# A first expert plan from nine of twelve token tiles, and four full expert tiles run while the last tokens are routed

## The reference

```
h = h + attn(layernorm(h))        # along axis 0 of 1536 tokens, 12 heads of 16
x = layernorm(h)
t = rmsnorm(x) * norm_scale
g = t @ gate_w.T + gate_b                 # 16 experts
top_vals, top_idx = top_k(g, 4)
route_w = softmax(top_vals)
hid = t @ mlp1_w + mlp1_b                 # 192 -> 768 per expert
a = glu * sigmoid(1.702 * glu) * (lin + 1)    # glu = min(., 7), lin = clip(., -7, 7)
y = a @ mlp2_w + mlp2_b                   # 384 -> 192
out = h + x + sum over the 4 experts of route_w * y
```

## Time and profile before

| what | value |
|---|---|
| median of 3 runs | 701.22 us (701.01 to 701.29) |
| profiled execution, own time | 701.36 us |
| its span, first to last instruction | 699.1 us |
| mean granted clock of PE | 0.955 of full |
| busy: PE, DVE, ACT, POOL | 618.1, 397.4, 382.1, 284.4 us |
| attention with its head start | from 213 to 432 us of the span |
| from attention's last matmul to the experts' first | 432 to 458 us |
| experts | 458 to 679 us |

### The profile page before, as it was taken

How to read it: one execution, slowest core, us unless ns; L and a number is a source line. 1 busy time by engine, 2 the same in 40 slices (tenths; PEclk the granted TensorE clock), 3 DMA queues, 4 the chain that set the end, 5 groups by cost and what they waited for, 6 DMA issues and landing times.

```text
span 699.1 us, 17374 instructions
## 1 busy us (share of the span) xinstructions
PE 618.1 (88%) x5055; PEld 424.5 (61%) x5056; DVE 397.4 (57%) x1418; ACT 382.1 (55%) x733; POOL 284.4 (41%) x340
## 2 busy tenths in 40 slices
PE   5888899889795999999999998579999999999980
PEld 5776687568662222222222323379999999999970
DVE  0445857775665236666666646636666666666650
ACT  0323347533334899999999997034444444444430
POOL 3122323321424034666666645603445353544451
PEclk9999999999997999999999999579999999999995
DMA  8999999700015525655565330289898998889944
GB/s 318 420 364 312 318 326 348 261 2 1 12 41 132 85 122 184 167 160 160 160 167 160 70 79 33 87 272 279 239 250 235 237 250 236 245 236 240 244 62 79
DMA packets 78193, 132.63 MB, mean 190 GB/s; under 512 B 36859, under 2 KB 62892, under 8 KB 76876
## 3 DMA queue, kind: packets, MB, share of 16 engines
q1 hardware_dynamic: 64892, 116.79, 53.7%
q0 software_dynamic: 11712, 14.19, 10.9%
q10 hardware_dynamic: 1552, 1.18, 0.5%
HBM read 105.53 MB, written 58.42 MB: 235 GB/s over the span
## 4 chain that ended last, share of the span: by engine, by line
PE 60%; DVE 15%; POOL 7%; issue 7%; ACT 5%; DMA 3%; SPq 1%; DVEq 0%; POOLq 0%; ACTq 0%
PE ps L1039 13%; PE ps L1068 8%; PE ps L1049 7%; PE ps L889 7%; PE ps L876 5%; PE ps L720 2%; PE ps L729 2%; POOL rstd L516 2%; DVE stat L1267 1%; ACT mid L1174 1%; DVE mid L1279 1%; PE ps L750 1%; ACT big L1174 1%; ACT big L1130 1%; PE ps L836 1%
## 5 line engine op out<-in xcount | busy, mean ns | idle before, releaser
L1174 ACT ACTIVATE mid<-ps 128x1536 f32<-128x1536 f32 x108 | 153.8, 1467 | 11.0 <-PE ps L876 10.4
L1039 PE MATMUL ps<-mid,big 128*128 128x128 f32 x756 | 99.2, 282 | 0.7 <-ACT mid L1200 0.7
L666 POOL DMA_INDIRECT out<-mid x32 | 49.6, 1550 | 118.4 <-ACT mid L1219 117.1
L876 PE MATMUL ps<-mid 52*128 52x512 f16 x432 | 86.5, 390 | 11.8 <-DMA mid<-big 5.6
L1039 PEld LDWEIGHTS ps<-mid,big 128*128 128x128 f32 x756 | 92.0, 194 | 5.0 <-ACT mid L1200 1.4
L1210 ACT ACTIVATE mid<-mid 128x384 f32<-128x384 f32 x63 | 33.0, 523 | 100.5 <-DVE mid L1618 100.5
L889 PE MATMUL ps<-mid 128*32 128x384 f32 x864 | 85.9, 501 | 0.0
L1618 DVE TENSOR_SCALAR mid<-ps,big 128x128 f32<-128x128 f32 x189 | 54.7, 345 | 48.0 <-issue 35.4
L1068 PE MATMUL ps<-big,mid 128*128 x378 | 67.5, 327 | 0.9 <-issue 0.5
L1068 PEld LDWEIGHTS ps<-big,mid 128*128 128x128 f32 x378 | 60.6, 190 | 1.7 <-issue 1.6
L876 PEld LDWEIGHTS ps<-mid 52*128 52x128 f16 x432 | 16.8, 94 | 72.8 <-ACT mid L1174 36.2
(11 more groups left out here) (232 smaller groups left out, 1073.1 us busy)
## 6 DMA issues: line engine op xcount, KB each, us to landing
big<-w_cat SPq DMA_DIRECT2D x63, 576.0 KB, 4.5
expert_in<-expert_in SPq DMA_DIRECT2D x16, 1774.5 KB, 46.4
big<-expert_in SPq DMA_DIRECT2D x63, 136.5 KB, 3.7
w_cat<-w_a SPq DMA_DIRECT2D x4, 1536.0 KB, 7.3
big<-w SPq DMA_DIRECT2D x2, 2304.0 KB, 8.9
big<-patches SPq DMA_DIRECT2D x8, 512.0 KB, 8.9
big<-patches SPq DMA_DIRECT2D x2, 2048.0 KB, 21.7
w_cat<-w_b SPq DMA_DIRECT2D x2, 1536.0 KB, 7.4
```

The source lines that it names most:

```text
L666: nc.gpsimd.indirect_dma_start(sums[r], bass.IndirectOffsetOnAxis(ap=tok_idx[q], axis=0), yt[q], None, compute_op=ALU.add).then_inc(y_out[ ...
L876: last = nc.tensor.matmul(SETS[kb % 2][:, c * 512:(c + 1) * 512], keysT[n_par][row:row + STK, kb * P:(kb + 1) * P], qrysT[n_par][row:row + ...
L1039: last = nc.tensor.matmul(banks[half][:, c * P:(c + 1) * P], w1_t[q][:, half * FF + c * P:half * FF + (c + 1) * P], xtT[r][:, 0:P], start= ...
L1174: nc.scalar.activation(probs[kb % 4], SETS[kb % 2], ACT.Exp, scale=0.5).then_inc(probs_ready, 1)
```

## The change

A first plan is made from the counts of token tiles 0 to 8. It lists four tiles of 128 rows (`T0 = 4`) that are already full then. They are loaded during the last attention tile and run between the end of attention and the rest of the plan; the late plan lists the other 59. There are still 63 expert tiles in all. `xtT`, `glu`, `lin`, `sig`, `actv` and `yt` move to other places in SBUF, as attention still uses the old ones; the biases use banks 5, 6 and 7; the sums of the first four tiles all go to `odd_sum`. The RMS norm's root is taken from the variance along with the layer norm's, in one power of two columns, so that the square and its sum fall away.

```
 def root_var(r):
-    step(tensor_scalar(vps[:, 0:1], var, 1e-5, None, ALU.add))
-    tensor_tensor(rstd[:, 0:1], vps[:, 0:1], nhalf[:, 0:1], ALU.pow)
+    tensor_scalar(vps[:, 0:1], var, LN_EPS, None, ALU.add)
+    step(tensor_scalar(vps[:, 1:2], var, 1.0 + RMS_EPS, LN_EPS * RMS_EPS, ALU.mult, ALU.add))
+    tensor_tensor(rstd[:], vps[:], nhalf[:, 0:2], ALU.pow)
-root_ms: one tensor_scalar and one pow on POOL; norm_square: square and reduce_sum on DVE
...
 DVE, behind dve_head(NT - 2):
+dve.wait_ge(plan_consts, 1)
+memset, then 15 instructions: full0 = counts of full tiles, ends0 = their running sum,
+at most T0; plan0_cols = expert and row                       -> plan0_cols_ready
 tT_copy(base)
 output(NT - 2, base + 1)
 choose(NT - 3, base + 2)
+first_tables(base + 3)                                        # -> plan0_ready
...
 norm_rows(NT - 1, 1, (NT - 1) // 2)
+clip_glu(0, 0)
 tT_copy(base + 1)
+clip_lin(0, 0)
 choose(NT - 1, base + 2)
+clip_act(0, 0)
 weigh(NT - 1, 1)
 place(NT - 1, 1, base + 3, cnt)
 the plan (two instructions more than before)                  # -> plan_cols_ready
+clip_glu(1, 1); clip_lin(1, 1); clip_act(1, 1)
 the tables                                                    # -> plan_ready
+clip_glu(2, 0); clip_lin(2, 0); clip_glu(3, 1); clip_lin(3, 1)
 six bias adds
+clip_act(2, 0); clip_act(3, 1)
...
 PE, last attention tile, behind the values of block 3:
+plan_transpose(plan0_cols, plan0_cols_ready, base + 3)
 PE, behind attention (all new order):
+x_transpose(0, 0, 16)
+comb_transpose(range(0, 4), 5)
+out_transpose(NT - 1, base - 1)
+x_transpose(1, 1, 16)
+ranks(NT - 2, base)
+comb_transpose(range(4, 8), 6)
+mlp1(0, 0, 16)
+mlp1(1, 1, 16, narrow_first=True)
+t_transpose(NT - 1, 1, base + 1)
+x_transpose(2, 2, 16); comb_transpose(range(8, 10), 5)
+logits(base + 2)
+x_transpose(3, 3, 16)
+mlp1(2, 2, 16)
+ranks(NT - 1, base + 3, counts=True)
+mlp2(0, 0)
+mlp1(3, 3, 16, narrow_first=True)                             # waits lin_ready >= 2
+mlp2(1, 1)
+comb_transpose(range(NT - 2, NT), 5)
+plan_transpose(plan_cols, plan_cols_ready, base + 4)
+six weighted_bias, the last three each wait for a bias add
+mlp2(2, 0); mlp2(3, 1)
+x_transpose(4, 0, 32); x_transpose(5, 1, 32); two_tiles(4, 0, 16); two_tiles(6, 2, 16)
...
 SP:
-sp.wait_ge(plan_ready, 1)
+sp.wait_ge(plan0_ready, 1)
 load_weights(0, 0)
+sp.wait_ge(rows_out[0], 16 * (TOPK * 5 + 1)); sp.wait_ge(rows_out[1], 16 * (TOPK * 4 + 1))
 rows and weights of tiles 0 to 3
+sp.wait_ge(plan_ready, 1); load_weights(NW, 0)
+wait for all rows_out, then tiles 4 and on
```

More of the change, by code:

```diff
@@ L48 @@
 HROW = P // 2
+T0 = NW
 DUMP = NT * P
@@ L317, in head_base, with plan_entry, x_bank, sum_of @@
             return 4 * n - 6 if not isinstance(n, int) or n >= 2 else 1
+        def plan_entry(first, late, j):
+            if isinstance(j, int) and j < T0:
+                return first[0:1, j:j + 1]
+            return late[0:1, bass.ds(j - T0, 1)]
+        def x_bank(j, q):
+            return 0 if isinstance(j, int) and j < T0 else 7 * (q % 2)
+        def sum_of(j):
+            return 1 if j < T0 else j % 2
+        def adds_to(s, j):
+            return sum(1 for i in range(j) if sum_of(i) == s)
         def held_wait(eng, s, value):
@@ L921, in ranks, with plan_transpose @@
                 last.then_inc(tr_ready, 1)
+            def plan_transpose(cols, ready, job):
+                pe.wait_ge(tr_taken, job)
+                pe.wait_ge(ready, 1)
+                for c in range(2):
+                    last = nc.tensor.matmul(b7[0:1, c * P:(c + 1) * P], cols[:, c:c + 1], ident[:], start=True, stop=True)
+                last.then_inc(tr_ready, 1)
             def pe_head(n, par, old=True, last=False):
@@ L974, in _, with comb_transpose @@
             pe_head(NT - 1, 1, last=True)
-            base = head_base(NT - 1) + 7
-            out_transpose(NT - 1, base - 1)
-            for t in range(NT - 2):
-                last = nc.tensor.transpose(ps[0:E, t * P:(t + 1) * P], comb_all[:, t, :], ident[:])
-            last.then_inc(combT_psum, 1)
-            ranks(NT - 2, base)
+            base = head_base(NT - 1) + 8
+            def comb_transpose(tiles, b):
+                for i, t in enumerate(tiles):
+                    last = nc.tensor.transpose(bank(b)[0:E, i * P:(i + 1) * P], comb_all[:, t, :], ident[:])
+                last.then_inc(combT_psum, 1)
             def weighted_bias(pair):
@@ L1215, in y_tile @@
                 if before is not None:
-                    act.wait_ge(y_out[q % 2], before)
+                    act.wait_ge(y_out[1 if isinstance(j, int) and j < T0 + NW else q % 2], before)
                 act.wait_ge(y_psum, j + 1)
@@ new lines, in _ @@
+            clip_glu(1, 1)
+            clip_lin(1, 1)
+            clip_act(1, 1)
+            dve.wait_ge(tr_ready, base + 5)
+            nc.vector.tensor_copy(ej_i, b7[0:1, 0:MT])
+            nc.vector.tensor_copy(row_i, b7[0:1, P:P + MT])
+            nc.vector.tensor_scalar(exrow_i, b7[0:1, 0:MT], float(P), None, ALU.mult).then_inc(tr_taken, 1)
+            dve.wait_ge(tr_taken, base + 5)
+            nc.vector.tensor_copy(bank_mark[:], ones[:, 0:1]).then_inc(plan_ready, 1)
+            clip_glu(2, 0)
@@ new lines, in _ @@
+            clip_lin(2, 0)
+            clip_glu(3, 1)
+            clip_lin(3, 1)
+            dve.wait_ge(base_ready, NT)
+            for t in range(0, NT, 2):
+                dve.wait_ge(bias_psum, t // 2 + 1)
+                pair = h_res[:, t:t + 2, :].rearrange("p t c -> p (t c)")
+                nc.vector.tensor_tensor(pair, pair, bank(BIAS_BANK[t // 2])[:, 0:2 * C], ALU.add).then_inc(bias_added, 1)
+            clip_act(2, 0)
+            clip_act(3, 1)
+            for j in range(T0, 2 * NW):
```

394 lines of the change are left out of this document (227 added, 167 removed).

## The result

The changed kernel takes 707.17 us (median of 4 runs, 704.70 to 708.83), the kernel before 701.25 beside it; the ratio is 1.0068, with a 95% interval from 1.0045 to 1.0091. It is slower by 0.7%, clear of noise. The profiled execution is the fastest of the four: 704.70 us, span 702.8, granted clock 0.961.

The account below looks back on a forecast made before the run. ACT was taken to pace attention, with PE nearly full, and PE the experts' steady part. 701.36 + 8.0 + 14.1 - 17.2 = 706.3, less 0.14 for the median: 706.1 us; range 699.5 to 711.5.

Parts of the forecast that it names:

- Term A: Last attention tile: its last PE matmul, called T, comes 8.0 us later, at least 5.3.
- the stall: Last attention tile: DVE's first plan, waiting for POOL's `edges`, delays out_transpose and leaves ACT idle, 4.8 us.
- the clock: Last attention tile: PE at half clock behind its idle time costs 2.7 us, between 0 and 5.
- Term B: Gap from T, attention's last PE matmul, to the first left-over expert tile: 14.1 us longer, at least 11.3 at full clock.
- The adds: In the gap: DVE's six bias adds, the last three waiting for banks of the first, take 3.5 us.
- mlp2(2) and (3): In the gap, behind clip_act(2): the second matmuls of expert tiles 2 and 3 take 1.95 us for both.
- Rival 3: PE at half clock through the whole gap: some 4 us more there, 2.5 more behind it, 712 us; chance 0.15.
- rival 1: The clock stays full in the last attention tile and the gap: 700.6 us, give or take 1.5; chance 0.2.
- Term C: Experts from the first left-over tile to tiles 8 and 9: 12.6 us instead of 29.8, saving 17.2 us.
- the norm is worth nothing in either place: Shorter routing norm gains nothing: beside ACT's exponentials in attention, or in the gap, where PE is busy until T + 7.75.
- wrong if T stays under 436: Sign against the forecast: attention's last PE matmul, expected at about 440 us in the trace, coming before 436.
- The table load: In the gap: ACT's 1.28 us load ahead of tile 0's swish makes DVE wait ahead of the last `weigh`.

Follow-up runs that it names:

- e8: The changed kernel with the routing norm of the kernel before, so the plan alone: 709.58 us, ratio 1.0104 to the kernel before.
- e1: The changed kernel with POOL making the table `edges` before attention instead of behind four indirect DMAs: 700.15 us, ratio 0.9968 to the kernel before.
- e3: The changed kernel with 36 unused identity transposes on PE ahead of the late out_transpose of token tile 10: 703.24 us, ratio 1.0014 to the kernel before.
- e2: The kernel before with only the routing norm changed to one power of two columns: 697.68 us, ratio 0.9940.
- e10: e9 with clip_act(0) behind the plan's columns, mlp2(0) behind the plan's transposes, third bias pair behind mlp1(3): 693.24 us, ratio 0.9890 to the kernel before.
- e9: e1 with half the biases early, mlp1(4) ahead of mlp2(2) and (3), and e4's edit: 691.15 us, ratio 0.9863 to the kernel before.
- e4: The changed kernel with the late plan's transpose ahead of mlp1(3) and DVE's tables ahead of tile 1's clips: 707.36 us, ratio 1.0077 to the kernel before.
- e12: e9 with 18 and 22 unused identity transposes in PE's idle time ahead of mlp1(3), two bias pairs behind them: 689.90 us, ratio 0.9818 to the kernel before.
- e11: e10 with unused identity transposes on PE ahead of mlp1(3), 30 before the first biases and 15 behind mlp2(0): 692.24 us, ratio 0.9866 to the kernel before.

## Why the prediction was right, and where it was not

**The sum held: 707.17 measured, 706.1 forecast.** But it held in part by luck: two of its errors cancelled, as the two halves show.

**Term A** (8.0 forecast). The mechanism was as told, from the IOTA to ACT's wait. ACT's waits in the last token tile grew from 0.7 to 7.8 us, by 7.1, in the changed kernel and in e8 alike. Against e1 the stall costs 4.0 us in the first wait (4.22 less 0.24) for 4.8 forecast, since the sixteen instructions took 2.7 us (415.21 to 417.92) and not 3.3; the clock costs 2.7 (e3) for 2.7; against before, the plan's transposes cost 0.42 for 0.5. Attention as a whole is 5.8 us longer in the changed kernel and 7.4 in e8: the difference is what the norm gives in the other token tiles.

**Term B** (14.1 forecast, 17.0 measured by the distance from T to mlp1(4)). Up to the bias adds the steps held: mlp1(3) took 4.3 us for 4.0, plan_ready was at T + 26.8 for 28.0, the first bias add at T + 31.9 for 32.5. Then two terms were mis-sized. The adds took 5.3 us (467.84 to 473.15), not 3.5: I counted waits for banks but not that PE makes each product at half clock. And mlp2(2) and (3) took 3.85 us, not 1.95. Rival 3, half clock through the whole gap, had 0.15. It came true in part: mlp2(1), the plan's transposes and the first three pairs of biases ran at full clock (1.14, 0.60 and 2.18 us), but from 467 to 477 us the clock was 0.50, and the two terms above add 3.7 us, where the rival had some 4 for the gap. mlp1(4) then ran at full clock, so that the 2.5 us that it added behind stayed away. The bound of 11.3 for B at full clock is not worked out in the prediction: mlp1(3) at full clock takes off 1.7 us, which gives 12.4, and rival 1 should have stood 1.1 us higher.

**Term C** (17.2 forecast): 29.83 less 12.28, 17.55.

**The step that failed** is "the norm is worth nothing in either place". It gave 0.0036 to 0.0060 of the time, 2.5 to 4.2 us (e8, e2). In the other token tiles I took ACT's exponentials to cover it, but ACT waited for scores there, and with the new norm these waits shrank from 3.1 to 1.7 us. In the gap I argued that PE, busy until T + 7.75, would hide the earlier row. PE, free at T + 6.9, did hide most of it: t_transpose came only 0.5 us sooner than in e8. What I left out is DVE's own order: clip_glu(0) stands behind the norm's rows, started 1.4 us sooner, and with it everything behind, up to mlp1(4), 2.1 us sooner than in e8. The plan alone costs 1.0104, 7.3 us; by the steps of the forecast it was 4.9. In e8's trace the excess is in B, 19.0 us (44.87 less 25.84) for 14.1. So the plan was underpriced by 2.4 us and the norm's gain left out, of about the same size.

**What would show it**: "wrong if T stays under 436". T was 435.97, and the step it guarded was right; the tokenizer ahead had run 1.9 us shorter. The bound belonged on a length, not on a time of the trace. The table load was forecast on the path and was: DVE waits 1.11 us for it. The Trainium skill's drain of 1.38 us ("ScalarE: Activation LUTs", What ACT_TABLE_LOAD costs) would by the prediction's estimate have made the gap 1.4 us longer; here the load begins at 445.61, when ACT's copy before it ends, and takes 1.28, and the swish starts at 446.90, 0.01 us behind it. The trace doesn't agree with a drain on either side of the load.

**What stays open**: how much the norm gives exactly: the profiles place 2.6 us in e2 and 3.6 between e8 and the changed kernel, the ratios say 4.2 and 2.5, and the intervals allow one value for all. And why the clock in e10 came back some 10 us later than in e9.

## What to carry to other kernels

Before a plan is pulled forward, see who makes what it reads and how late that engine comes to it: twelve columns of constants behind four indirect DMAs cost more here than the whole slowdown. A wait that hides behind another shows no gain when it is removed first (e4) and 2 to 3 us when it is removed last (e9), so try such edits again after each step. Price PE's work behind an idle stretch at half clock, and measure the parts of a change apart, since a sum can be right by errors of opposite sign.

## What the hardware did that I had not expected

Work that nothing uses paid: 40 transposes of the identity, 4.8 us of PE's time, made e12 faster than e9 (ratio 0.9818 for 0.9863; tile 8 2.5 us sooner, granted clock 1.00 against 0.85 to 0.86 in the gap). And an edit that brought the plan 1.5 us sooner (e10) had tile 8 3.5 us later in the profiled execution, 2.9 of which came back when PE was kept at work in nearly the same order (e11); the times of e10's runs alone, 2.1 us above e9's by the median, are not clear of noise.
